# Decoder block on one core: half of the cross-attention key norms as a quadratic form, two products per group, summed on VectorE

## What is computed

```python
q = (hidden_states @ Wq).reshape(B, Sq, H, D)
k = (encoder_hidden_states @ Wk).reshape(B, Skv, H, D)
q = rmsnorm(q, gq)      # x * rsqrt(mean(x*x) + 1e-5) * g
k = rmsnorm(k, gk)
scores = jnp.einsum('bqhd,bkhd->bhqk', q, k) * scale
```

## Time and profile before

| | us |
|---|---|
| median of 3 runs | 1323.64 |
| lowest and highest run | 1322.04, 1323.68 |
| span of the profiled execution, first to last instruction | 1321.1 |
| PE / DVE / ACT / POOL busy in it | 1290.7 / 1155.3 / 1074.3 / 1089.0 |

### The profile page before, as it was taken

One profiled execution on the slowest core, in us unless ns is written; L12 is line 12 of the kernel. 1 busy time (PEld: TensorE's weight loads), 2 busy tenths in 40 slices (PEclk: granted clock), 3 DMA queues, 4 the chain that ended last, 5 costly groups with the idle time before them and its releaser, 6 DMA issues.

```text
span 1321.1 us, 21768 instructions
## 1 busy us (share of the span) xinstructions
PE 1290.7 (98%) x6516; PEld 1059.3 (80%) x6516; DVE 1155.3 (87%) x1777; ACT 1074.3 (81%) x3171; POOL 1089.0 (82%) x922
## 2 busy tenths in 40 slices
PE   8989999999999999999999999999999999999998
PEld 5767677788888888888888888888888888878787
DVE  5866689999999999999999999999999999997755
ACT  2667788899999999999999999999899999973442
POOL 5644452989999999999999999999999999999840
PEclk9989999999999999999999999999999999999999
DMA  7140230101010101010101010101010101030300
GB/s 254 46 160 1 80 136 13 36 13 36 13 36 12 36 12 36 13 36 13 36 13 36 13 36 13 35 13 36 13 36 10 38 9 40 1 112 1 115 24 29
DMA packets 27845, 54.12 MB, mean 41 GB/s; under 512 B 2816, under 2 KB 22400, under 8 KB 25936
## 3 DMA queue, kind: packets, MB, share of 16 engines
q1 hardware_dynamic: 26736, 52.38, 11.8%
q10 hardware_dynamic: 992, 0.36, 0.1%
HBM read 44.60 MB, written 8.13 MB: 40 GB/s over the span
## 4 chain that ended last, share of the span: by engine, by line
PE 83%; ACT 5%; DVE 5%; POOL 4%; issue 3%; ACTq 0%; POOLq 0%; DVEq 0%
PE xa_k_ps L1419 12%; PE xa_k_ps L1420 11%; PE xa_k_ps L1421 11%; PE xa_s_ps L1420 5%; PE xa_s_ps L1421 5%; PE xa_s_ps L1419 5%; PE xa_o_ps L1419 5%; PE xa_o_ps L1421 4%; PE xa_o_ps L1420 4%; PE om_ps L1516 3%; PE xa_o_ps L1510 3%; PE xq_ps L634 2%; POOL xa_den L1170 1%; POOL probs_r L1184 1%; DVE xa_ss L1349 1%
## 5 line engine op out<-in xcount | busy, mean ns | idle before, releaser
L1349 DVE TENSOR_REDUCE xa_ss<-xa_sq 125x6 f32<-125x768 f32 x360 | 339.5, 943 | 3.7 <-ACT xa_sq L1267 2.2
L1184 POOL TENSOR_TENSOR probs_r<-probs,xa_p_hi 125x896 fp32r<-125x896 f32 (+1 forms) x160 | 330.4, 2065 | 5.3
L1419 PE MATMUL xa_k_ps<-wk_parts,xa_ctxT_hi 128*125 128x512 f32 x768 | 324.0, 422 | 6.2 <-ACT xa_sq L1267 5.9
L1420 PE MATMUL xa_k_ps<-wk_parts,xa_ctxT_hi 128*125 128x512 f32 x768 | 302.8, 394 | 0.0
L1421 PE MATMUL xa_k_ps<-wk_parts,ctxT_lo 128*125 128x512 f32 x768 | 302.4, 394 | 0.0
L1336 DVE TENSOR_TENSOR xa_scores<-xa_s_ps,xa_rk 125x448 f32<-125x448 f32 x384 | 237.8, 619 | 50.8 <-PE xa_s_ps L1421 48.4
L1170 POOL TENSOR_TENSOR xa_den<-probs,xa_den 125x896 f32<-125x896 f32 x128 | 272.8, 2131 | 3.7 <-ACT probs L1248 3.7
L1226 ACT ACTIVATE xa_sq<-xa_k_ps 125x512 f32<-125x512 f32 x360 | 213.8, 594 | 26.0 <-DVE xa_ss L1349 16.6
L1248 ACT ACTIVATE probs<-xa_scores 125x896 f32<-125x896 f32 x192 | 182.8, 952 | 57.0 <-POOL xa_scores L1159 35.1
L1266 ACT ACTIVATE xa_k_ps<-xa_k_ps 125x128 f32<-125x128 f32 x720 | 193.9, 270 | 21.6 <-PE xa_k_ps L1421 21.3
L1357 DVE TENSOR_TENSOR xa_max_ps<-xa_scores,xa_max_ps 125x448 f32<-125x448 f32 x320 | 198.1, 619 | 0.6
(11 more groups left out here) (187 smaller groups left out, 2479.1 us busy)
## 6 DMA issues: line engine op xcount, KB each, us to landing
xa_ctx_nat<-in_ctx SPq DMA_DIRECT2D x16, 750.0 KB
ctxT_in<-in_ctxT SPq DMA_DIRECT2D x84, 125.0 KB, 2.1
qo<-in_xo_w SPq DMA_DIRECT2D x1, 2048.0 KB, 16.7
qo<-in_xq_w SPq DMA_DIRECT2D x1, 2048.0 KB, 15.3
vo_scratch<-qo SPq DMA_DIRECT2D x2, 1024.0 KB, 4.0
w_parts_scratch<-ws_hi SPq DMA_DIRECT2D x2, 1024.0 KB, 4.1
w_parts_scratch<-ws_lo SPq DMA_DIRECT2D x2, 1024.0 KB, 5.3
vo<-vo_scratch SPq DMA_DIRECT2D x1, 2048.0 KB, 8.8
```

The source lines that it names most:

```text
L1184: pool.tensor_tensor(probs_r[0:KP, slots, :], probs[0:KP, slots, :], p_hi[:, y // 2 % (NPR // 2), first:2, :].bitcast(F32), ALU.subtract). ...
L1349: dve.tensor_reduce(ss[:, i // 2, UH * (i % 2):UH * (i % 2) + vector_heads(of)], squares(of, i).rearrange("p (g d) -> p g d", d=XD), AX.X, ...
L1419: pe.matmul(out, l_hi, r_hi, start=first, stop=False)
L1420: pe.matmul(out, l_hi, r_lo, start=False, stop=False)
```

## The change

For heads 0 to 3 and 8 to 11 the key's square sum is no longer made from the key. With G = Wk_h Wk_h' (128 by 128) it is c'Gc. `gram` makes these eight G on PE in the query path, and they take the place of those heads' columns in `wk_hi` and `wk_lo`. The first projection of a step is then (rounded c) times (G high + G low), two products where there were three. DVE multiplies its result elementwise with m = 2c - (rounded c) and sums along each head: four `tensor_tensor_reduce` of 125 by 128 a step, with one sum each. The result differs from c'Gc by a term of second order in c's rounding. m comes from a new tile `ctx_m`, loaded by SP in three parts of four tiles a phase, rounded by ACT (`round_m`) and combined by DVE (`double_m`). The `tensor_reduce` of line 1349 and the squares of lines 1226 and 1267 go; ACT takes all four heads of the second bank with `accum_out`. In DVE's list the sums stand first in a step, ahead of the scaling of the scores. The first bank is freed by DVE (`formed`) in place of ACT.

```diff
+        GRAM_AT, GRAM_BANKS, GRAM_HEADS = (V, V + 1), (0, 3), (0, UH)
...
+            def gram(i):
+
+                pe.wait_ge(qn_ready, V - 3 if i == 0 else V)
+                for g in range(QH):
+                    head = wkT[:, GRAM_HEADS[i] + g, :]
+                    mm = pe.matmul(ps[:, GRAM_BANKS[i], g * C:(g + 1) * C], head, head, start=True, stop=True)
+                mm.then_inc(gram_mm, 1)
+
             for v in range(LAST):
                 if v < V:
                     project(v)
+                if v in GRAM_AT:
+                    gram(GRAM_AT.index(v))
...
-WH = 6
+GH = 4
 QC = 4
 HALF = 0.5 * XD ** -0.5
+MEAN = HALF / XD
+MT = 4
+M_HI_AT = {3: (0, 2), 11: (1, 0), 19: (1, 1)}
+M_AT = {6: (0, 2), 14: (1, 0), 22: (1, 1)}
...
-def vector_heads(ph):
-
-    return UH if ph.b == -1 else WH
+def m_part(at, ph, j):
+
+    if j not in at:
+        return None
+    ahead, part = at[j]
+    to = ph.shift(ahead)
+    return (to, part) if to.within(0, B - 2) else None
...
+            def load_m(ph, part):
+
+                wait(sp, formed, ph.at(STEPS, 2 * MT * (part + 1)) if ph.b >= 0 else 0)
+                src = a.ctx[ph.b + 1].rearrange("(p t) c -> p t c", t=KT)
+                sp.dma_start(m_tiles(part), src[:, MT * part:MT * (part + 1), :]).then_inc(m_loaded[part], 16)
+
+                    load_m(ph.shift(1), 0)
...
+                        if c == 1:
+                            load_m(ph.shift(1), 1)
...
+                    load_m(ph.shift(1), 2)
+                if ph.b == -1:
+                    for part in range(KT // MT):
+                        load_m(Phase(0), part)
...
+                        if part < 2:
+                            mlp.store_parts(sp, part)
...
+            def round_m(ph, part):
+
+                act.wait_ge(m_loaded[part], 16 * (ph.b + 2))
+                wait(act, m_ready, m_count(ph, part) - 1)
+                act.activation(m_hi[:, :, :], m_tiles(part), ACT.Copy).then_inc(m_hi_ready, 1)
...
-                    if ph.within(-1, 14):
-                        wait(act, k_done, ph.at(2 * STEPS, 2 * STEPS + 2 * j + 1))
-                        wait(act, summed, ph.at(STEPS, STEPS + j - 1))
-                        act.activation(squares(ph, j)[:, 0:4 * XD], k_ps[0:KP, (2 * j) % 3, :], ACT.Square
-                                       ).then_inc(squared, 1)
+                    if m_part(M_HI_AT, ph, j):
+                        round_m(*m_part(M_HI_AT, ph, j))
...
-                        own = vector_heads(ph) - 4
                         act.wait_ge(k_done, ph.at(2 * STEPS, 2 * STEPS + 2 * j + 2))
-                        for g in range(own, 4):
-                            head = UH * (j % 2) + 4 + g
+                        for g in range(UH - GH):
+                            head = UH * (j % 2) + GH + g
                             cols = k_ps[0:KP, (2 * j + 1) % 3, g * XD:(g + 1) * XD]
-                            act.activation(cols, cols, ACT.Square, accum_out=ss[:, j // 2, head:head + 1])
-                        act.activation(squares(ph, j)[:, 4 * XD:(4 + own) * XD],
-                                       k_ps[0:KP, (2 * j + 1) % 3, 0:own * XD], ACT.Square).then_inc(squared, 1)
+                            last = act.activation(cols, cols, ACT.Square, scale=MEAN ** 0.5,
+                                                  accum_out=ss[:, j // 2, head:head + 1])
+                        last.then_inc(squared, 1)
...
+                if c in (-6, -4, -2):
+                    round_m(Phase(-1), (c + 6) // 2)
                 if 0 <= c < 4:
-                    if c == 0:
+                    part = slice(c * 512, (c + 1) * 512)
+                    if c % 2 == 0:
+                        act.wait_ge(query.gram_mm, c // 2 + 1)
+                        act.activation(wk_hi[:, part], query.gram_ps(c // 2), ACT.Copy).then_inc(wk_hi_ready, 1)
...
+            def double_m(ph, part):
+
+                dve.wait_ge(m_hi_ready, m_count(ph, part))
+                dve.scalar_tensor_tensor(m_tiles(part), m_tiles(part), 2.0, m_hi[:, :, :].bitcast(F32),
+                                         ALU.mult, ALU.subtract).then_inc(m_ready, 1)
...
+                    if ph.within(-1, 14):
+                        if j % (2 * MT) == 0:
+                            dve.wait_ge(m_ready, m_count(ph, j // (2 * MT)))
+                        dve.wait_ge(k_done, ph.at(2 * STEPS, 2 * STEPS + 2 * j + 1))
+                        for g in range(GH):
+                            cols = k_ps[0:KP, (2 * j) % 3, g * C:(g + 1) * C]
+                            head = UH * (j % 2) + g
+                            form = dve.tensor_tensor_reduce(cols, cols, ctx_m[:, j // 2, :], MEAN, 0.0, ALU.mult, ALU.add,
+                                                            ss[:, j // 2, head:head + 1])
+                        form.then_inc(formed, 1)
...
-                    if (ph.within(-1, 14) and j >= 1) or (ph.within(0, 15) and j == 0):
-                        i = (j - 1) % STEPS
-                        of = ph if j >= 1 else ph.shift(-1)
-                        dve.wait_ge(squared, ph.at(2 * STEPS, 2 * STEPS + 2 * j))
-                        dve.tensor_reduce(ss[:, i // 2, UH * (i % 2):UH * (i % 2) + vector_heads(of)],
-                                          squares(of, i).rearrange("p (g d) -> p g d", d=XD), AX.X, ALU.add
-                                          ).then_inc(summed, 1)
+                    if m_part(M_AT, ph, j):
+                        double_m(*m_part(M_AT, ph, j))
...
-                            dve.wait_ge(summed, ph.at(STEPS, STEPS + KT if ahead else STEPS))
-                            dve.scalar_tensor_tensor(ss[:, g, :], ss[:, g, :], HALF / XD,
+                            dve.wait_ge(formed, ph.at(STEPS, STEPS + KT if ahead else STEPS))
+                            dve.wait_ge(squared, ph.at(STEPS, STEPS + KT if ahead else STEPS))
+                            dve.scalar_tensor_tensor(ss[:, g, :], ss[:, g, :], 0.0,
                                                      max_ps[0:KP, UW:UW + 1].unsqueeze(2)
-                                                     .broadcast_to([KP, KT // 2, XH]), ALU.mult, ALU.add
+                                                     .broadcast_to([KP, KT // 2, XH]), ALU.max, ALU.add
...
+                if c in (-5, -3, -1):
+                    double_m(Phase(-1), (c + 5) // 2)
...
+                    dve.tensor_tensor(wk_lo[:, part], query.gram_ps((c - 1) // 2) if c % 2 else wk_in[:, part],
+                                      wk_hi[:, part].bitcast(F32), ALU.subtract).then_inc(wk_lo_ready, 1)
...
-                return three(k_ps[0:KP, (2 * j + c) % 3, :], ctxT_hi[:, i, t, :], ctxT_lo[:, i, t, :],
-                             wk_hi[:, cols], wk_lo[:, cols])
+                out = k_ps[0:KP, (2 * j + c) % 3, :]
+                if c == 0:
+                    pe.matmul(out, ctxT_hi[:, i, t, :], wk_hi[:, cols], start=True, stop=False)
+                    return pe.matmul(out, ctxT_hi[:, i, t, :], wk_lo[:, cols], start=False, stop=True)
+                return three(out, ctxT_hi[:, i, t, :], ctxT_lo[:, i, t, :], wk_hi[:, cols], wk_lo[:, cols])
...
-                        wait(pe, squared, ph.at(2 * STEPS, 2 * STEPS + 2 * j - 2))
+                        wait(pe, squared, ph.at(STEPS, STEPS + j - 1))
...
-                        wait(pe, squared, ph.at(2 * STEPS, 2 * STEPS + 2 * j - 1))
+                        wait(pe, formed, ph.at(STEPS, STEPS + j))
```

More of the change, by code:

```diff
@@ L737, in query_path @@
         path = Arrays()
+        path.gram_mm, path.gram_ps = gram_mm, lambda i: ps[:, GRAM_BANKS[i], :]
         path.sync, path.tensor, path.gpsimd, path.scalar, path.vector = sync, tensor, gpsimd, scalar, vector
@@ L1015, in probs_pair, with m_tiles, m_count @@
             return probs[0:KP, y % NPR:y % NPR + 2, :]
[L1017 to L1021, removed]
+        def m_tiles(part):
+            return ctx_m[:, MT * part:MT * (part + 1), :]
+        def m_count(ph, part):
+            return KT // MT * (ph.b + 1) + part + 1
         wk_hi_ready, wk_lo_ready, ones_set = (
@@ L1028, in cross_attention @@
         qhi_ready, qlo_ready = sem("xa_qhi_ready"), sem("xa_qlo_ready")
-        k_done, squared, summed = sem("xa_k_done"), sem("xa_squared"), sem("xa_summed")
+        k_done, squared, formed = sem("xa_k_done"), sem("xa_squared"), sem("xa_formed")
+        m_loaded = [sem(f"xa_m_loaded{i}") for i in range(KT // MT)]
+        m_hi_ready, m_ready = sem("xa_m_hi_ready"), sem("xa_m_ready")
         mean_ready, ln_ready, table_ready, rk_ready = (
@@ L1081, in body @@
                     sp.dma_start(vo[:, :, :], a.vo).then_inc(vo_loaded, 16)
-                    sp.wait_ge(summed, STEPS * B)
+                    sp.wait_ge(formed, STEPS * B)
                     mlp.load_x1(sp)
@@ L1090, in body @@
                     mlp.load_w2(sp)
-                if ph.b == -1:
-                    mlp.store_parts(sp)
             attention.sync(sp)
```

(13 more changed lines are left out.)

28 lines of the change are left out of this document (14 added, 14 removed).

## The result

The changed kernel takes 1372.61 us (median of 4 runs, 1372.48 to 1372.92) beside 1323.66 us for the kernel before (4 runs, 1322.04 to 1323.95): ratio 1.0372, 95% interval 1.0357 to 1.0386. It is slower by 49 us; 1392 was forecast. The span of its profiled execution is 1370.7 us, 49.6 us over that of before.

What follows compares the result with a forecast made beforehand. PE was the bound at 65.65 us a phase, DVE 3.9 behind; DVE becomes it at 41.2 + 25.2 + 2.1 + 1.8 = 70.3. 15 x (70.3 - 65.65) = +70, edges -1, hence 1392 us; range 1315 to 1510.

Steps and rivals of the forecast that it cites:

- Each sign named for "right": Phases 0 to 14: DVE near 99%, PE 85 to 90%, 96 accumulator reads a phase, products 0.26 us apart.
- The sums: DVE, each phase: 96 product-and-sums at 0.263 us, product 0.198 plus 0.065 for the sum, 25.2 us added.
- The middle of the bounds: DVE's price for one sum: 0.065 us taken, between floor 0, ACT's 0.14 and at most 0.19.
- rival b: DVE's accumulator read waits for the product to drain, as on ACT: 0.338 us each, 1501 us; chance 0.22.
- rival c: DVE's product-and-sum at half rate, or its read at full 0.19: 0.39 us each, about 1580 us; chance 0.05.
- rival a: DVE's sum needs no instruction of its own: 0.198 us each, faster at 1300 us; chance 0.15.
- The order: DVE, sums first: the maximum waits right behind the scaling, 17 bubbles of 0.125 us, 2.1 us a phase.
- m (1.8 us): DVE, each phase: three `double_m` of 512 columns at 0.60 us each, 1.8 us added.
- the upper end: Top of the range 1315 to 1510 us; `double_m` waiting out POOL, up to 6 us a phase, kept for it.
- What stays: DVE's work a phase without the 24 reductions: 61.8 - 20.6 = 41.2 us.
- The edges: Outside the 15 phases: phase -1 -3.5 us, query path +2.5 us, moved store and m loads nothing; together -1 us.

Runs made afterwards that it cites:

- the run with POOL relieved: Changed kernel with one plain product a step in place of four product-and-sums, and most of GpSimd's denominator additions at half the columns: 1289.19 us, ratio 0.9742.

## Why the prediction was right, and where it was off

**The side and the cause: right.** DVE was named as the new bound at 70.3 us a phase, PE at 59.6. Measured: DVE busy 99% of phases 0 to 14, a middle phase of 69.7 us, PE's loads waiting for DVE's sums, and PE's saving nearly worthless (9.7 us of 83). Each sign named for "right" is there: 1536 accumulator reads in 16 phases (96 each), products 0.25 us apart, and the maximum 0.65 to 0.67 us after the scaling in 17 steps a phase. Only PE stands at 92%, above the 85 to 90% named. Its busy time counts modelled ends: a product lasts 0.39 us where the next can start after 0.23, so each halt hides some 0.16 us. Counted by starts (an estimate, 0.23 us for 512 columns and in proportion), PE is held up for 11.5 us of the 69.7 from 703 us on, which leaves 58 us of work, near the 59.6.

**The sums (96 x 0.263 = 25.2 us): too high by 2.4.** Measured 24 x 0.95 = 22.8. The step that a sum costs one more short instruction of 0.065 us had the instruction right but not that the next product starts together with the read. What it costs is 0.04 us: 0.25 from start to start behind a read, 0.21 without one. The middle of the bounds was still the right choice: the mean of 0.238 us excludes ACT's 0.14 on top (rival b, 0.338), half rate (rival c) and the sum for nothing in a row of four (rival a, 0.198); only the first product of a step, 0.21, comes near the last.

**The order (2.1 us): right in size, incomplete.** 0.65 in place of 0.53 us was there, 24 x 0.087 = 2.1 a phase. That the other order has its price as well wasn't considered: the maximum behind a read takes 0.04 us more, and DVE meets PE's scores and POOL's instructions at other times.

**m (1.8 us): less than half of what it costs.** Measured 3 x 1.26 = 3.8 us. The row behind 0.60 us, 150.79 to 152.08, was taken where POOL stood idle; POOL's own row beside it says so:

```profile
152.40 0.72 POOL L1113 TENSOR_TENSOR ctxT_lo<-ctxT_in,xa_ctxT_hi 128x250 fp32r<-128x250 f32 x1 [5.76 <-ACT xa_ctxT_hi L1214]
```

The forecast named the right mechanism (a `double_m` that must wait out a POOL instruction of 2.1 us) but kept it for the upper end, though POOL was busy 92% of phases 0 to 14: the expected wait was worked out nowhere. It would have been about 0.92 x 2.1 / 2 = 1.0 us each, an estimate for starts at any place in POOL's instruction; measured 0.66 here and 0.96 with the sums second, since the starts fall at the same three places in every phase. At the 0.60 us forecast, 45 of them (phases 0 to 14) would take 45 x 0.66 = 30 us less, which puts the kernel near 1343; the run with one operand in PSUM gave 1342, with 42 of them and fewer columns. Even at 0.60 us each the kernel would so be slower than before. The half rate that the Trainium skill ("Vector Engine (DVE) Microarchitecture Reference", section "Points that are easy to get wrong") states was rightly left out of the sum: no run shows it, since `double_m` takes 0.69 us alone with 512 columns and 0.54 to 0.56 behind POOL.

**What stays (41.2 us): right in size.** 69.7 - 22.8 - 2.1 - 3.8 = 41.0, of which 0.7 is DVE's idle time. It was worked out from the mean of 15 phases, though, and this is a middle one.

**From a phase to 15: the larger part of the 19 us.** That the phase came out so near (70.3 for 69.7, 0.6 x 15 = 9 us) is luck: the sums were 2.4 us too high and m 2.0 too low, 36 and 30 us over the 15 phases. Another 13.5 us came from `15 x (70.3 - 65.65)`: phases 0 and 14 are shorter than the middle ones, before and after, so the mean of before held two short phases and the 70.3 us was multiplied by all 15. 13 x 69.7 + 60.0 + 66.0 = 1032; 15 x 69.7 = 1045.5. The edges took 3.4 us back.

**The edges (-1 us): measured +2.4.** The query path took 1.6 us more (the first key product starts at 154.97 us, before at 153.35), where 2.5 were forecast, and the end 1.0 less. Phase -1 didn't give its 3.5 us: up to the first scaled sums it took 1.8 longer. PE there is down to 31.35 of 34 us, but ACT has 29.4 and DVE 25.4, none is full. The store of the split weights behind a load of m was costed at nothing, and the trace shows one way in which it wasn't. Before, then after:

```profile
170.37 0.61 POOL L1653 CAST ws_hi<-ws_raw 128x512 fp32r<-128x512 f32 x1 [2.32 <-DMA w_parts_scratch<-ws_hi]
```

```profile
174.88 0.61 POOL L1716 CAST ws_hi<-ws_raw 128x512 fp32r<-128x512 f32 x1 [5.26 <-DMA w_parts_scratch<-ws_hi]
...
179.06 0.71 POOL L1152 TENSOR_TENSOR ctxT_lo<-ctxT_in,xa_ctxT_hi 128x250 fp32r<-128x250 f32 x1
...
179.87 0.47 PE L1490 MATMUL xa_k_ps<-wk_parts,xa_ctxT_hi 128*125 128x512 f32 x1 [1.52 <-POOL ctxT_lo L1152]
```

The first store is issued at 167.59 us, 1.6 later than before (166.01), right behind a load of m (167.22). But POOL, which waits for it, goes on 4.5 us later than before, and PE then waits 1.5 us for POOL's low part. That is about the 1.8 us; no run took it away, so its share stays open.

**Rival (a)** had a cap that this kernel doesn't reach: with nothing to pay on DVE, PE's saving brings 14 to 16 us (1308 and 1309), not 24. POOL ends it in part, as the run with POOL relieved shows; that the handovers between four engines at 91 to 96% do the rest is argued, not shown.

## What to carry to other kernels

A DVE instruction with both operands in SBUF beside a busy GpSimd costs its own time plus what is left of GpSimd's instruction: price it by GpSimd's busy share and the length of its instructions (here 1.0 us for measured 0.66 and 0.96), or place one operand in PSUM. An engine's saving is worth only what the others have room for; with the others at 91 to 94%, a twelfth of the bound's work was worth 14 us of 83 even for nothing. When a stretch repeats with shorter ends, compare a middle repeat with a middle repeat.

## What the runs showed of the hardware that had not been expected

- A DVE instruction with two SBUF operands waits out the POOL instruction that it meets: 41 of 41 `double_m` end 0.54 to 0.56 us after it, and so do 14 of 14 plain subtractions; POOL's next takes 0.22 to 0.44 us longer in the mean.
- A product-and-sum of 128 columns with its accumulator read costs DVE 0.21 us, then 0.25 us in a row; the read, 0.14 us long, lies beside the next product. ACT's costs 0.29 us.
- Right behind a DVE accumulator read an instruction that writes to PSUM takes 0.04 us more, and one that writes to SBUF doesn't. Durations with the sums second, 300 to 1100 us: the maximum into `max_ps` (PSUM) 0.661 us behind a read (195 of them) and 0.616 otherwise (34), the same maximum into `cmax` (SBUF) 0.610 behind a read (23). The products, in place in PSUM, have 0.327 and 0.284; the scaling, into SBUF, 0.622 and 0.611.
